# The next tile's token-shift block issued earlier on VectorE, and two normalisation operations moved from GpSimd to VectorE, in an eight-core RWKV and local-attention kernel

## What is computed

```python
xx = shift(x) - x                       # shift: the token before
xxx = x + xx * tmx
t5 = tanh(xxx @ maa_w1)                 # (T, 5, 32)
m = einsum('btfe,fec->fbtc', t5, maa_w2)
xw, xk, xv, xr, xg = (x + xx * (tm_f + m[f]) for f in range(5))
r, k, v, g = xr @ Wr, xk @ Wk, xv @ Wv, silu(xg @ Wg)
w = tdecay + tanh(xw @ td_w1) @ td_w2; decay = exp(-exp(w))
# recurrence over t for each head: y = r (S + u kv); S = decay * S + kv
yn = (y - mean(y)) / sqrt(var(y) + EPS) # per head
yn = yn * ln_w + ln_b
out = yn * g @ Wo
```

## Time and profile before

| | us |
|---|---|
| median of two timed runs (4697.6 to 4702.72) | 4700.16 |
| the profiled execution | 4691.85 |
| its span on core 0, the slowest | 4690.3 |

### The profile page before, as it was taken

The page is one execution under the profiler, slowest core; times in us unless marked ns, Lnnn a source line. Parts: engine busy times, 40 slices in busy tenths (PEclk is TensorE's granted clock), DMA queues, the critical chain, the costliest instruction groups (busy, mean ns, idle before and its releaser), DMA issues.

```text
span 4690.3 us, 40134 instructions; the slowest of 8 cores (4652.9 to 4690.3 us)
## 1 busy us (share of the span) xinstructions
PE 2384.1 (51%) x11904; PEld 1127.4 (24%) x11904; DVE 1856.7 (40%) x4397; ACT 854.9 (18%) x1814; POOL 141.1 (3%) x92
## 2 busy tenths in 40 slices
PE   1445444566311124444544699782544445797850
PEld 0222222232111112211211244331211111343320
DVE  4554455444356642334245412122333435321243
ACT  2233233222100001212221211001121221111010
POOL 0000000000022210000000000000000000000000
PEclk9656565677655557765656799886666556898975
DMA  5100000300322214000003031323000002223224
GB/s 120 45 10 10 10 18 10 54 27 19 80 45 45 45 43 85 0 0 1 1 1 52 14 72 51 84 74 46 1 0 0 1 16 41 51 63 79 74 74 166
DMA packets 181684, 190.83 MB, mean 41 GB/s; under 512 B 77696, under 2 KB 139520, under 8 KB 181440
## 3 DMA queue, kind: packets, MB, share of 16 engines
q1 hardware_dynamic: 139648, 131.67, 9.2%
q0 software_dynamic: 41824, 56.59, 7.8%
HBM read 184.00 MB, written 60.82 MB: 52 GB/s over the span
## 4 chain that ended last, share of the span: by engine, by line
PE 42%; DVE 26%; issue 10%; ACT 9%; DMA 8%; POOL 3%; DVEq 1%; SPq 0%; ACTq 0%; POOLq 0%
PE ps L1348 11%; PE ps L1418 7%; PE ps L1039 4%; ACT arena_b L1146 4%; PE pw L1139 4%; DVE arena_b L430 3%; PE pw L577 2%; PE ps L400 2%; PE ps L509 2%; DMA arena_b<-w2p 2%; DMA arena_f<-s_d 2%; PE pw L1210 2%; PE pw L1165 2%; DVE arena_f L772 1%; PE pw L874 1%
## 5 line engine op out<-in xcount | busy, mean ns | idle before, releaser
L1348 PE MATMUL ps<-arena_b 128*128 128x512 bf16 x2816 | 640.3, 392 | 63.1 <-DVE arena_b L1363 63.1
L1348 PEld LDWEIGHTS ps<-arena_b 128*128 128x128 bf16 x2816 | 281.3, 100 | 428.2 <-issue 117.5
L1418 PE MATMUL ps<-arena_b 128*128 128x512 bf16 x1408 | 314.3, 387 | 105.8 <-DMA arena_b<-w2p 105.8
L1151 DVE TENSOR_TENSOR arena_b<-arena_b,arena_f 128x128 bf16<-128x128 bf16 x448 | 130.5, 292 | 511.0 <-ACT arena_b L1146 509.7
L1139 PE MATMUL pw<-arena_b 64*128 64x128 bf16 (+1 forms) x448 | 185.5, 418 | 281.0 <-ACT arena_b L1146 279.7
L1363 DVE SCALAR_TENSOR_TENSOR arena_b<-ps,arena_f,arena_b 128x512 bf16<-128x512 f32 x176 | 131.6, 750 | 474.3 <-ACT arena_b L1358 419.9
L1039 PE MATMUL ps<-arena_b 128*128 128x512 bf16 x768 | 189.4, 407 | 166.4 <-DVE arena_b L1027 134.2
L1146 ACT ACTIVATE arena_b<-pw 128x128 bf16<-128x128 f32 (+1 forms) x448 | 195.4, 438 | 395.7 <-PE pw L1139 395.6
L1358 ACT ACTIVATE arena_b<-ps,arena_f 128x512 bf16<-128x512 f32 x176 | 121.0, 687 | 541.1 <-PE ps L1348 538.3
L430 DVE SCALAR_TENSOR_TENSOR arena_b<-arena_f 128x256 bf16<-128x256 f32 x320 | 153.1, 478 | 138.3 <-ACT arena_f L425 138.1
L1418 PEld LDWEIGHTS ps<-arena_b 128*128 128x128 bf16 x1408 | 139.9, 100 | 280.3 <-issue 120.7
(11 more groups left out here) (177 smaller groups left out, 3197.7 us busy)
## 6 DMA issues: line engine op xcount, KB each, us to landing
h_d<-arena_b SPq DMA_DIRECT2D x176, 128.0 KB, 1.8
arena_b<-h_d SPq DMA_DIRECT2D x16, 1408.0 KB, 6.1
arena_f<-x SPq DMA_DIRECT2D x32, 512.0 KB, 5.0
arena_b<-w1p POOLq DMA_DIRECT2D x4, 3072.0 KB, 22.9
arena_b<-w2p POOLq DMA_DIRECT2D x4, 2816.0 KB, 23.4
arena_b<-w1p POOLq DMA_DIRECT2D x4, 2560.0 KB, 27.6
arena_b<-rq_d SPq DMA_DIRECT2D x16, 512.0 KB, 4.9
s_d<-arena_f SPq DMA_DIRECT2D x16, 512.0 KB, 2.7
```

The costliest lines, as they stand in the source:

```text
L1151: p.emit("vector", lambda v, ab_=ab_, oo=oo, mko=mko, msk=msk: v.tensor_tensor(ab_[:, oo + mko: oo + mko + 128], ab_[:, oo + mko: oo + mko ...
L1348: last = t.matmul(pb.ap()[:], wb[:, k * 1536 + (2 * pi + agi) * 128: k * 1536 + (2 * pi + agi) * 128 + 128], z1[:, k * T + tt4 * 512: k * ...
L1418: last = t.matmul(pb.ap()[:], wb2[:, k * C + ctO * 128: k * C + ctO * 128 + 128], hs[:, k * 512:(k + 1) * 512], start=(k == 0), stop=(k == ...
```

## The change

- The block (L385, L389) becomes a function of its own, `emit_xxx(it, pass2)`. It is emitted for tile 0 ahead of each pass, and for tile it+1 inside `tile_pass(it)`: in pass 1 after the decay stage and ahead of the key stage, in pass 2 after the last L435 and ahead of the value matmuls L577.
- The guards by parity on `xxx` and `t5f` go; a new guard `xxxbuf`, set after a tile's t5mm, protects the single `xxx` buffer.
- In phase2 the operations of L826 and L828 are emitted on VectorE instead of GpSimd.

```diff
-        def tile_pass(it, pass2):
+        xxx_done_t = {}
+
+        def emit_xxx(it, pass2):
             t0 = it * TS
...
-                p.emit("vector", lambda v, ct=ct, t0=t0: v.scalar_tensor_tensor(
-                    xxx[:, ct * TS:(ct + 1) * TS], xx[:, ct * TS:(ct + 1) * TS],
+                p.emit("vector", lambda v, ct=ct, t0=t0, xx=xx: v.scalar_tensor_tensor(
+                    xxx1[:, ct * TS:(ct + 1) * TS], xx[:, ct * TS:(ct + 1) * TS],
                     self.vecs["tmx"][:, ct:ct + 1], self.xn_view(ct, t0, TS),
-                    ALU.mult, ALU.add), waits=G(("xxx", par, ct)) + [(sv, None)], incs=[(sv, 1)])
-            xxx_done = sv.n
+                    ALU.mult, ALU.add), waits=G(("xxxbuf",)) + [(sv, None)], incs=[(sv, 1)])
+            xxx_done_t[it] = sv.n
+
+        def tile_pass(it, pass2):
...
+            xxx_done = xxx_done_t[it]
             for f5 in range(5):
...
-                    waits=[(sm, None)] + G(("t5f", par, f5)), incs=[(sa, 1)])
+                    waits=[(sm, None)], incs=[(sa, 1)])
                 SG(("t5ps", f5 % 2), sa)
+            SG(("xxxbuf",), sm)
...
                     SG(("qlb",), sa)
+                if it + 1 < NTIL:
+                    emit_xxx(it + 1, pass2)
                 for ct in range(8):
                     pb = self.ps[2 + ct % 2]
                     ob1 = oper[1]
...
             else:
+                if it + 1 < NTIL:
+                    emit_xxx(it + 1, pass2)
                 for fi, (f, dst, silu) in enumerate(((2, fV, False), (4, fG, True))):
...
+        emit_xxx(0, False)
         for it in range(NTIL):
             tile_pass(it, pass2=False)
...
+        emit_xxx(0, True)
         for it in range(NTIL):
             tile_pass(it, pass2=True)
...
-            p.emit("gpsimd", lambda g_: g_.tensor_tensor(ysb, sqb, self.lnw_rep, ALU.mult),
-                   waits=[(sv, None), (sl, None), (self.sem("p2_lnr"), 32)], incs=[(sl, 1)])
-            p.emit("gpsimd", lambda g_: g_.tensor_tensor(sqb, ysb, self.lnb_rep, ALU.add),
-                   waits=[(sl, None)], incs=[(sl, 1)])
+            p.emit("vector", lambda v: v.tensor_tensor(ysb, sqb, self.lnw_rep, ALU.mult),
+                   waits=[(sv, None), (sl, None), (self.sem("p2_lnr"), 32)], incs=[(sv, 1)])
+            p.emit("vector", lambda v: v.tensor_tensor(sqb, ysb, self.lnb_rep, ALU.add),
+                   waits=[(sv, None)], incs=[(sl, 1)])
```

More of the change, by code:

```diff
@@ L370, in phase1 @@
         zro_t = s_zro.n
-        def tile_pass(it, pass2):
+        xxx_done_t = {}
+        def emit_xxx(it, pass2):
             t0 = it * TS
-            c0g = (it * TS) // L
-            G = self.guard; SG = self.set_guard
+            G = self.guard
             par = it % 2
             xx = xx2[par]
-            xxx = xxx1
-            t5f = t5f1
             for ct in range(8):
@@ L388, in tile_pass @@
                     waits=w0, incs=[(sv, 1)])
-                p.emit("vector", lambda v, ct=ct, t0=t0: v.scalar_tensor_tensor(
-                    xxx[:, ct * TS:(ct + 1) * TS], xx[:, ct * TS:(ct + 1) * TS],
+                p.emit("vector", lambda v, ct=ct, t0=t0, xx=xx: v.scalar_tensor_tensor(
+                    xxx1[:, ct * TS:(ct + 1) * TS], xx[:, ct * TS:(ct + 1) * TS],
                     self.vecs["tmx"][:, ct:ct + 1], self.xn_view(ct, t0, TS),
-                    ALU.mult, ALU.add), waits=G(("xxx", par, ct)) + [(sv, None)], incs=[(sv, 1)])
-            xxx_done = sv.n
+                    ALU.mult, ALU.add), waits=G(("xxxbuf",)) + [(sv, None)], incs=[(sv, 1)])
+            xxx_done_t[it] = sv.n
+        def tile_pass(it, pass2):
+            t0 = it * TS
+            c0g = (it * TS) // L
+            G = self.guard; SG = self.set_guard
+            par = it % 2
+            xx = xx2[par]
+            xxx = xxx1
+            t5f = t5f1
+            xxx_done = xxx_done_t[it]
             for f5 in range(5):
@@ L563, in tile_pass @@
                     SG(("fRQ", ct), sst); SG(("fKK", ct), sst)
-                    SG(("xx", par, ct), sl); SG(("xxx", par, ct), sm)
-                for f5 in range(5):
-                    SG(("t5f", par, f5), sm)
-            else:
+                    SG(("xx", par, ct), sl)
+            else:
+                if it + 1 < NTIL:
+                    emit_xxx(it + 1, pass2)
                 for fi, (f, dst, silu) in enumerate(((2, fV, False), (4, fG, True))):
```

## The result

| | before | after |
|---|---|---|
| median of all timed runs | 4707.05 us (10) | 4585.73 us (11) |
| ratio of the comparable runs | | 0.9736, 95% interval 0.9718 to 0.9754 |
| span of the slowest core in the profile | 4690.3 us (core 0) | 4586.1 us (core 1) |

The account below looks back on a forecast made before the run. No engine was busy all the time; the edits aimed at serial waits of PE (143.7 us) and DVE (83.4 us). 39 + 83 + 1, 124 us unrounded, off the 4690.3 us span, plus 9.9 us, gave 4576 us (4550 to 4608).

Parts of the forecast that it names:

- recurrence: Normalisation in each of 16 chunks: two operations on DVE instead of GpSimd save 2.45 us a chunk, 39 us.
- pass 2: Seven tile boundaries: block fits DVE's idle time, t5mm starts 10.01 us earlier and warm; net 11.9 us each, 83 us.
- pass 1: Seven tiles: 7.8 us gained at the boundary, 7.6 us lost in the key stage; about +1 us in all.
- The warm start: Pass 2, t5mm straight after L577 runs at the high clock: five groups take 4.35 us, 2.7 us less.
- the counter value taken at emission: Pass 1 key stage: L495's wait takes DVE's count after the block's increments, so it starts 7.02 us late.
- Pass 1 gains too: Rival, chance 0.04: the exponential doesn't wait for the block, PE keeps 7.81 us in pass 1; 4523 us.
- Pass 2 gains nothing: Rival, chance 0.04: another wait stands right behind, say the store of v_d and g2x_d before L588; 4659 us.
- The dense stages lose the high clock: Rival, chance 0.03: matmuls such as L1348 and L1418 turn slow, 0.205 us each; at one in four, 4792 us.
- The level of 13/16: Skill's rule: a current limit cuts a die's clock to 13/16 when three of its cores run dense matmuls.

Follow-up runs that it names:

- narrow: Changed kernel, but the key stage's ACT exponential waits only for the scans' count taken before the block is emitted; pass 1 722.8 us, ratio to before 0.9683.
- spread: Changed kernel, but pass 1's block is cut into eight pairs, each behind a first exponential of the receptance stage; ratios to before 0.9624 and 0.96.
- p2_only: Changed kernel with pass 1's block back at its tile's head and the two recurrence operations back on GpSimd; pass 2 263.4 us, no ratio.

## Why the prediction was right

The forecast was 4576 us (4550 to 4608); 0.9736 times 4700.16 us is 4576 us. That it agrees to the microsecond is luck, since the interval of the ratio alone is 4568 to 4585 us; but the total didn't come right by one stage making up for another, each holds by itself:

| term | forecast | measured in the stages |
|---|---|---|
| recurrence | 39.2 us | 37.9 us |
| pass 2 | 83.3 us | 84.8 us |
| pass 1 | 1.4 us | 0.3 us |
| sum | 124 us | 123.0 us (124.4 us from the start to the end of the recurrence) |

- **Recurrence.** The two operations take 1.226 us each, so the price taken from L830 was exact. The gap was undersized in one place: L842 starts 0.18 us after L840's end instead of 0.10 us, which is the missing 0.08 us x 16 = 1.3 us. Its wait names the semaphore that GpSimd counts up too; that this is the reason isn't shown.
- **Pass 2.** The mechanism is as forecast, three sizes are off by some tenths. In the mean over all cores and the seven boundaries, the idle time gained is 10.2 us (forecast 10.0). The warm start gives 6.45 - 4.27 = 2.2 us from the first to the last t5mm start (forecast 2.7): the tile from which the 2.7 us were read was one of the slower ones, others took as little as 5.6 us. The matmuls of L577, first to last start, take 15.4 us before and 15.6 us after, a cost of 0.2 us (forecast 0.8); after the change they alternate between about 15 and 16.4 us, as the clock's rise falls early or late (3.7 and 5.9 us after the start in two tiles in a row on core 1, which take 15.4 and 16.5 us). 10.2 + 2.2 - 0.2 = 12.2 us against the 11.9 us forecast (the stage gained 84.8 / 7 = 12.1 us). So here two errors, 0.5 us too much for the warm start and 0.6 us too much for its cost, do cancel.
- **Pass 1.** The step that mattered was that of the counter value taken at emission. Three key groups, then a stop, a gap of 5.71 us ("about 6"), a wait of 6.91 us (7.02), a restart at the low clock and a rise 4.9 us later (5.1): each is in the rows. From the end of the last decay copy to the first L534 it takes 17.8 us; before, from L471's end to L522, 10.0 us: 7.8 us late against the 7.6 us of the forecast, and 7.8 us gained at the boundary. Over all cores and tiles it is 17.85 us against 9.84 us, 8.0 us late, and t5mm, for which the forecast had no change in this pass, gives 0.4 us back (6.14 us from first to last start instead of 6.52 us). `narrow` and `spread` show that the place of the block was the cause: with the wait narrowed 14.2 us come back, with the block elsewhere 50 to 52 us.
- **The rivals.** "Pass 1 gains too" was worth 53 us and failed on the wait that spoke against it, and its price was wrong: it took the wait for the only thing that holds PE, but without it `narrow` gets only 14.2 us, because DVE's first product is queued behind the block as well. `spread` reaches the 53 us by another place for the block. "Pass 2 gains nothing": ACT's value copies wait for PE (50.9 us in 15 waits, 54.2 us in 16 before) and never for the stores of v_d and g2x_d; one wait, of 4.8 us, is for a store of pass 1 (kk_d), ahead of the first copy of pass 2, and at no boundary. "The dense stages lose the high clock": they take the same time as before (392 and 387 ns in the earlier trace rows):

```profile
L1360 PE MATMUL ps<-arena_b 128*128 128x512 bf16 x2816 | 643.2, 393 | 74.1 <-DVE arena_b L1375 74.1
L1430 PE MATMUL ps<-arena_b 128*128 128x512 bf16 x1408 | 312.4, 386 | 117.5 <-DMA arena_b<-w2p 117.5
```

  The level of 13/16 that the prediction names beside this rival is in no record of this profile, but the profile of `p2_only` has it: 0.8125 in 14 to 21 records on each of cores 0 to 3, none on cores 4 to 7. There the matmuls of L589 took 465 ns on core 2, against 416 ns in the profile of after.
- **The range** allowed for 37 us between cores. In the first pair of profiles the rest of the program brought 18 us in one direction, enough to make the 4586.1 us look like a missing term.

## What to carry to other kernels

Idle time that is filled at one place can reappear at the next wait that names "everything emitted so far": before moving work earlier in an in-order queue, list what is queued behind it and which counts are taken after it, and put it where its engine waits for something else in any case. Of two operations on a slow engine, move the one with nothing beside it and leave the one that overlaps. When three stages are changed at once, cut the span at their ends and read each by itself: here a total of 104 us in one pair of profiles was 124 us in the changed stages, less some 20 us by which the untouched rest of these two executions differed.

## What the runs showed of the hardware

- Work that follows dense matmuls without a gap starts at the high clock (1.00 across the seam in pass 2), and the same 40 matmuls take 4.54 us instead of 7.06 us. Closing a gap ahead of a short matmul group can give back more than the gap, where what stands ahead is dense: in pass 1 of `spread` the gap is closed too, the stage ahead ran at 0.50, and the 40 matmuls take 7.09 us. I had the first in the sum, but not that the clock also rises *inside* a following idle stretch (0.74 in 450 to 457 us), where nobody has use for it.
- The untouched rest of the program, 2953 us at the shortest, took up to 19 us longer in other executions, at the same two clock levels; before the change and after it alike, by the timed runs.
